# Decoder layer with a mixture of experts on one core: VectorE's order in the first mixture pass, and the last sum read from PSUM

## The chip, the cores and the metric

The kernel runs on one core of one Trainium2 chip. The metric is the device time of one execution in microseconds (us). Five engines run their own queues in order and wait for each other by semaphores: TensorE (PE, with PEld for the loading of its weights), VectorE (DVE), ScalarE (ACT), GpSimd (POOL) and SyncE (SP), which issues most of the transfers.

## The reference

8 sequences of 512 tokens, 256 features. Self attention, cross attention, then a mixture of experts, each followed by a layer norm of input plus output. The last third is what the change touches:

```python
scores = softmax(x @ gate_w.T)                       # 8 experts
topk_w, topk_idx = top_k(scores, 2); topk_w /= topk_w.sum(-1)
pos = cumsum(one_hot(topk_idx.reshape(-1)), 0) - 1   # place of a token in its expert's queue
keep = pos_tok < capacity                            # 1.25 * N * K / E
y  = sum over experts of comb * (silu(x @ wg.T) * (x @ wu.T)) @ wd.T
sh = silu(x @ ws_gate.T) * (x @ ws_up.T) @ ws_down.T # two shared experts' worth, 512 wide
x = layernorm(x + y + sh)
```

## The kernel before

After the two attention layers (up to about 1251 us of the span) `moe_phase` works in three parts.

**The first mixture pass** walks over the 8 blocks (sequences) i = 0 to 7. Each block is a "job" of the first shared expert. TensorE turns the block's tokens (`turn`, into `ps_t`, in two halves f), multiplies for gate and up in two halves c (`gate_up(i, 0)`, `gate_up(i, 1)`, 12 matmuls of 512 columns each, into `ps_gu`), makes the routing scores of the next block (`score(i + 1)`, 24 matmuls of 8 columns) and then `down(i)` (24 matmuls of 256 columns, into `ps_dn`). All values are split into a high and a low part: ScalarE writes the high part (`x_hi`, `h_hi`, `split_hi` for weights), VectorE the rest (`x_lo`, `h_lo`, `split_lo`). The weights of three more experts are split in blocks 1 to 3 by VectorE and behind blocks 0 to 2 by ScalarE. For half c VectorE forms `product(i, c)` (silu(gate) times up), ScalarE `h_hi(i, c)`, VectorE `h_lo(i, c)`; only then may `down` run. `choose(i + 1)` on VectorE is the choice of two experts from the scores (19 small steps, with one exponential on ScalarE between two table loads), and `place(i)` turns the counts that TensorE made (`count`) into places in the experts' queues (10 small steps, semaphore `step_done`). GpSimd then scatters the block's tokens to `slots_x` in memory by 8 indirect transfers, and SP loads a later block into the same buffer (`HELD` = 3 buffers). ScalarE's `keep(i)` copies `ps_dn` to `ym`, from where SP stores it.

**The chunks.** Jobs 8 and 9 are the second shared expert for blocks 6 and 7. Then 40 chunks of 256 gathered tokens follow; the first (`chunk_turn(0)`) needs the scatter of block 7 and its load into `xs`. TensorE puts `chunk_turn(0)` between `down(8)` and `down(9)`.

**The last pass** is jobs 10 to 15 (`LATE` = 10), the second shared expert for blocks 0 to 5, and the final layer norm of 8 sums, n = 0 to 7 (n = 0 and 1 belong to jobs 8 and 9, n = 2 to 7 to jobs 10 to 15). GpSimd's `both(n)` adds two loaded parts into `totals`; VectorE's `moments(n)` adds the job's output in two halves ("pairs", 128x512 each), takes statistics of each 256 columns and aggregates them; GpSimd computes the scale and shift (`rstd`, `shift`), ScalarE's `norm(n)` applies them and SP stores. GpSimd runs `both(n + 3)` right behind the scale of n. In VectorE's queue `moments` stands behind each half job from (12, 1) on. TensorE's queue is gate_up(j, 0), gate_up(j, 1), down(j - 1). Each half of `down(j)` waits until ScalarE's `keep` has emptied that half of `ps_dn`:

```python
                        after(pe, ym_done, out_of_job(j - 1, pair) if j else 0)
```

## Time and profile before

| | |
|---|---|
| median of 3 runs | 1666.03 us (1665.53 to 1670.77) |
| profiled execution | 1674.12 us, span 1672.3 us, mean granted clock of TensorE 0.935 |
| PE busy | 1497.8 us (90%) |
| DVE busy | 1127.0 us (67%) |
| ACT busy | 922.1 us (55%) |
| POOL busy | 449.3 us (27%) |
| chain that ended last | PE 18%, DVE 4%, issue 1%, ACT 1% of the span |

Busy time is a share over the whole span. The change touches the stretches from 1265 to 1402 us (first pass) and from 1610 us to the end (last pass), and only the rows of these say what it is worth. The profiled execution's own time is 1.8 us above its span and 8.1 us above the median of the runs.

### The profile page before, as it was taken

To read this page: it belongs to the slowest core of one execution; us is meant where nothing else is said; L and a number is where in the kernel's file an instruction comes from. 1 tells how busy PE (TensorE), PEld (TensorE's weight loads), DVE (VectorE), ACT (ScalarE), POOL (GpSimd) and SP (SyncE) were. 2 spreads that over 40 slices of the span, in tenths; PEclk is the share of its full clock that TensorE was granted. 3 is DMA by queue.
4 is the path that set the end of the run, shared out by engine and by line. 5 is a ranking of instruction groups with operands and counts; after the bars stand their busy time and mean duration, and the time that the engine had idled before them with its cause. 6 is when DMAs were issued, how large, how long until landed. Compare 5 with 4: busy or idle time off the path is not lost. (4 is left out here: it accounts for less than half of the span.)

```text
span 1672.3 us, 27139 instructions
## 1 busy us (share of the span) xinstructions
PE 1497.8 (90%) x8424; PEld 991.3 (59%) x8424; DVE 1127.0 (67%) x2282; ACT 922.1 (55%) x1710; POOL 449.3 (27%) x412
## 2 busy tenths in 40 slices
PE   3887999999999999999999999986957899999993
PEld 2435555546555555554655555544437789999983
DVE  4736678778778868877877887845625664555557
ACT  3352566656656656665666665660624554555544
POOL 6013032013014103201301310101002543666664
PEclk8696999999999999999999999997967789999997
DMA  3616545554356455545535644506104534777662
GB/s 117 114 55 120 121 94 109 115 108 106 65 126 116 78 115 105 107 106 111 111 65 136 123 67 97 106 2 120 21 24 150 184 121 139 131 155 149 122 189 101
DMA packets 103990, 179.80 MB, mean 108 GB/s; under 512 B 14144, under 2 KB 59840, under 8 KB 101824
## 3 DMA queue, kind: packets, MB, share of 16 engines
q1 hardware_dynamic: 89280, 159.09, 42.5%
q0 software_dynamic: 14592, 19.41, 6.5%
q8 instruction: 42, 0.69, 0.2%
q14 instruction: 76, 0.62, 0.2%
HBM read 98.09 MB, written 79.30 MB: 106 GB/s over the span
## 5 line engine op out<-in xcount | busy, mean ns | idle before, releaser
L509 DVE TENSOR_REDUCE nm<-ps_max 128x1 f32<-128x512 f32 x1024 | 647.4, 682 | 179.3 <-PE ps_max L694 164.7
L469 ACT ACTIVATE prob<-ps_sc 128x512 f32<-128x512 f32 x1024 | 557.9, 597 | 333.6 <-PE ps_sc L707 319.2
L707 PE MATMUL ps_sc<-qk 128*128 128x512 f32 x1024 | 454.4, 447 | 47.1 <-DMA qk<-mst 30.6
L694 PE MATMUL ps_max<-qk 96*128 96x512 f32 x1024 | 428.8, 428 | 25.5 <-DVE nm L509 13.8
L707 PEld LDWEIGHTS ps_sc<-qk 128*128 128x128 f32 x1024 | 194.9, 192 | 342.6 <-ACT prob L469 276.3
L724 PE MATMUL ps_out<-prob,va 128*32 128x512 f32 x2048 | 277.7, 615 | 3.1 <-ACT prob L469 2.8
L694 PEld LDWEIGHTS ps_max<-qk 96*128 96x128 f32 x1024 | 204.4, 200 | 77.5 <-DVE nm L509 42.0
L1453 PE MATMUL ps_gu<-x2f,we 128*128 128x256 f32 (+1 forms) x1344 | 219.6, 318 | 4.0 <-ACT sg L1121 2.4
L1453 PEld LDWEIGHTS ps_gu<-x2f,we 128*128 128x128 f32 x1344 | 187.2, 189 | 20.7 <-ACT sg L1121 2.8
L351 POOL TENSOR_TENSOR rstd<-mv,eps 128x2 f32<-128x2 f32 x32 | 6.3, 197 | 652.6 <-DVE mv L578 652.6
L1453 PE MATMUL ps_dn<-we,hf 128*128 128x256 f32 x864 | 127.4, 305 | 22.3 <-DVE hf L1353 22.3
L1453 PEld LDWEIGHTS ps_dn<-we,hf 128*128 128x128 f32 x864 | 121.3, 213 | 23.9 <-DVE hf L1353 23.3
L614 PE MATMUL ps_job<-xf,w 128*128 128x512 f32 x288 | 81.8, 423 | 24.1 <-POOL xf L326 18.9
L724 PEld LDWEIGHTS ps_out<-prob,va 128*32 128x32 f32 x2048 | 40.6, 108 | 94.7 <-issue 68.6
L614 PE MATMUL ps_job<-w,cf 128*128 128x256 f32 x576 | 82.0, 295 | 5.7 <-DVE cf L495 3.6
L1045 POOL DMA_INDIRECT slots_x<-x2in,scat x64 | 65.4, 1022 | 79.7 <-issue 42.1
L614 PEld LDWEIGHTS ps_job<-w,cf 128*128 128x128 f32 x576 | 78.2, 201 | 9.6 <-DVE cf L495 4.2
L614 PEld LDWEIGHTS ps_job<-xf,w 128*128 128x128 f32 x288 | 55.6, 201 | 39.1 <-issue 20.6
L335 POOL TENSOR_TENSOR res<-res,trig 128x512 f32<-128x512 f32 x32 | 41.0, 1280 | 139.6 <-DVE res L526 139.6
L1059 POOL DMA_INDIRECT sums<-ys,dest x40 | 62.2, 1555 | 48.2 <-DVE dest L1389 24.9
L1059 POOL DMA_INDIRECT x<-ys,dest x40 | 62.0, 1550 | 31.4 <-ACT ys L1188 17.3
L326 POOL TENSOR_TENSOR xf<-raw,xf 128x1024 fp32r<-128x1024 f32 x8 | 21.4, 2674 | 146.7 <-ACT xf L381 146.7
(145 smaller groups left out, 1491.5 us busy)
## 6 DMA issues: line engine op xcount, KB each, us to landing
qk<-hbm_self SPq DMA_DIRECT2D x192, 128.0 KB, 5.3
hbm_self<-stage SPq DMA_DIRECT2D x16, 1024.0 KB, 4.0
qk<-hbm_cq SPq DMA_DIRECT2D x96, 128.0 KB, 5.0
qk<-hbm_ck SPq DMA_DIRECT2D x96, 128.0 KB, 5.5
slots_x<-zeros SPq DMA_DIRECT2D x8, 1360.0 KB, 5.8
xs<-slots_x SPq DMA_DIRECT2D x40, 272.0 KB, 3.9
weraw<-w_moe SPq DMA_DIRECT2D x11, 768.0 KB, 4.4
hbm_ck<-stage SPq DMA_DIRECT2D x8, 1024.0 KB, 4.4
```

Of the source, the lines that this page charges most:

```text
L326: nc.gpsimd.tensor_tensor(out, value, high.bitcast(F32), ALU.subtract).then_inc(lo_done[kind], 1)
L335: nc.gpsimd.tensor_tensor(rot[:, c, :], rot[:, c, :], trig[:, 1, :], ALU.mult) \
L351: nc.gpsimd.tensor_tensor(rstd[:, at, :], mv[:, at, 1:2], eps[:, at, :], ALU.add) \
L469: nc.scalar.activation(prob[:, s % 2, j, :], ps_sc[:, (HG * s + j) % NSC, :], ACT.Exp, scale=HD ** -0.5).then_inc(exp_done[a], 1)
L509: nc.vector.tensor_reduce(nm[:, g % 2, r:r + 1], ps_max[:, n % NMX, :], axis=AX.X, op=ALU.max, negate=True).then_inc(max_done[a], 1)
L614: ins = nc.tensor.matmul(out, l(a), r(b), start=(n == 0 and k == 0), stop=(n == len(pairs) - 1 and k == len(parts) - 1))
L694: nc.tensor.matmul(ps_max[:, n % NMX, :], qk[0:96, 0, h, P * c:P * c + P], qk[0:96, 1, h, :], start=True, stop=True).then_inc(smax_done[a], 1)
L707: nc.tensor.matmul(ps_sc[:, n % NSC, :], qk[:, 1, h, P * c:P * c + P], qk[:, 0, h, :], start=True, stop=True).then_inc(st_done[a], 1)
L724: ins = nc.tensor.matmul(ps_out[32 * j:32 * j + 32, :], va[:, a, c, HG * g + j, :], prob[:, s % 2, j, :], start=(c == 0), stop=(c == TT - ...
L1045: nc.gpsimd.indirect_dma_start(rows_x, bass.IndirectOffsetOnAxis(ap=scat[:, q, c, t:t + 1], axis=0), xin[:, q, t, :], None, bounds_check=P ...
L1059: nc.gpsimd.indirect_dma_start(x2 if j // NCH else sums, bass.IndirectOffsetOnAxis(ap=dest[:, c, t:t + 1], axis=0), ys[:, c, t, :], None, ...
L1453: ins = nc.tensor.matmul(o, l(a), r(b), start=(n == 0 and k == 0), stop=(n == len(pairs) - 1 and k == len(parts) - 1))
```

## The change

In the first pass `place(i)` is cut in two on VectorE: `take_counts(i)` (two small steps that read the counts from PSUM) stays behind `h_lo(i, 0)`, and the other nine steps, with `split_lo` behind them, come after `product(i, 1)` and `h_lo(i, 1)`.

In the last pass a table sets where `moments(n)` and `norm(n)` stand. n = 4 to 7 no longer go through ScalarE and `ym`: VectorE adds `ps_dn` straight into `totals`, and `down(j)` for j = 13 to 15 waits for that add of job j - 1 (`total_done`) where it waited for ScalarE's copy (`ym_done`).

```diff
+MOMENTS_AT = {(12, 0): 0, (12, 1): 1, (13, 0): 2, (13, 1): 3, (14, 0): 4, (15, 0): 5, (15, 1): 6}
+NORM_AT = {(12, 1): 0, (13, 0): 1, (13, 1): 2, (14, 0): 3, (14, 1): 4, (15, 1): 5}
...
-                    if pair == 0 and j >= B + MARGIN:
-                        act.wait_ge(total_done, 2 * (j - MARGIN - B + 1))
...
-                    n = 2 * (j - LATE - 2) + c - 2
-                    if n >= 0 and c == 0:
-                        norm(n)
-                if j > LATE:
-                    keep(j - 1)
-                if n >= 0 and c == 1:
-                    norm(n)
-            keep(NJ - 1)
+                    if c == 1 and LATE < j <= B + MARGIN:
+                        keep(j - 1)
+                    if (j, c) in NORM_AT:
+                        norm(NORM_AT[j, c])
...
                 h_lo(i, 0)
+                take_counts(i)
+                product(i, 1)
+                h_lo(i, 1)
                 place(i)
                 if 1 <= i < 4:
                     split_lo(i, i % 2, i)
-                product(i, 1)
-                h_lo(i, 1)
...
+                    if n < MARGIN:
+                        dve.wait_ge(ym_done, out_of_job(B + n, pair))
+                        nc.vector.tensor_tensor(mine, mine, ym[:, (B + n) % MARGIN, 2 * pair:2 * pair + 2, :],
+                                                ALU.add).then_inc(total_done, 1)
+                    else:
+                        dve.wait_ge(dn_done, of_job(B + n, pair))
+                        flat = mine.rearrange("p t d -> p (t d)")
+                        nc.vector.tensor_tensor(flat, ps_dn[:, pair, :], flat, ALU.add).then_inc(total_done, 1)
...
-                    n = 2 * (j - LATE - 2) + c - 1
-                    if n >= 0:
-                        moments(n)
+                    if (j, c) in MOMENTS_AT:
+                        moments(MOMENTS_AT[j, c])
...
-                        after(pe, ym_done, out_of_job(j - 1, pair) if j else 0)
+                        if j > B + MARGIN:
+                            pe.wait_ge(total_done, 2 * (j - 1 - B) + pair + 1)
+                        else:
+                            after(pe, ym_done, out_of_job(j - 1, pair) if j else 0)
```

VectorE's queue in a block of the first pass, before, from `h_lo(i, 0)` on (`h<-ps_gu,sg` is `product`, `hf<-h,hf` is `h_lo`, the rows of `r`, `prod`, `scat` and `tok` are `place`):

```order
L1353 TENSOR_TENSOR hf<-h,hf 128x512
L1322 TENSOR_TENSOR r<-ps_t,carry 128x32
L1323 TENSOR_TENSOR carry<-carry,ps_t 128x8
L1324 TENSOR_SCALAR r<-r 128x32
L1325 TENSOR_TENSOR r<-r,idx 128x32
L1326 TENSOR_TENSOR r<-r 128x32
L1327 TENSOR_TENSOR prod<-choice,r 128x64
L1331 TENSOR_REDUCE place<-prod 128x8
L1335 CAST scat<-place 128x8
L1337 COPY x2in<-r 128x4x8
L1338 COPY x2in<-tok 128x4
L1339 TENSOR_SCALAR tok<-tok 128x4
```

The same place of the queue in the changed kernel (its lines are numbered anew, L1317 and L1318 are the two steps that read the counts):

```order
L1353 TENSOR_TENSOR hf<-h,hf 128x512
L1317 TENSOR_TENSOR r<-ps_t,carry 128x32
L1318 TENSOR_TENSOR carry<-carry,ps_t 128x8
L1349 TENSOR_TENSOR h<-ps_gu,sg 128x512
L1353 TENSOR_TENSOR hf<-h,hf 128x512
L1324 TENSOR_SCALAR r<-r 128x32
```

`product(i, 1)` and `h_lo(i, 1)` now stand ahead of nine of the steps; before they stood behind all of them.

VectorE's queue in the last pass of the changed kernel, from `product(14, 0)` to `h_lo(15, 0)` (`totals` are the sums, `st` and `mv` the statistics); before, a `moments` with `totals<-totals,ym` stood behind each of the pairs `h`, `hf`, behind (14, 1) too:

```order
L1349 TENSOR_TENSOR h<-ps_gu,sg 128x512
L1353 TENSOR_TENSOR hf<-h,hf 128x512
L1432 TENSOR_TENSOR totals<-ps_dn,totals 128x512
L1435 BN_STATS st<-totals 128x6 x2
L1432 TENSOR_TENSOR totals<-ps_dn,totals 128x512
L1435 BN_STATS st<-totals 128x6 x2
L1440 BN_AGGR mv<-st 128x2 x4
L1349 TENSOR_TENSOR h<-ps_gu,sg 128x512
L1353 TENSOR_TENSOR hf<-h,hf 128x512
L1349 TENSOR_TENSOR h<-ps_gu,sg 128x512
L1353 TENSOR_TENSOR hf<-h,hf 128x512
```

The rows are `moments(4)`, then the half jobs (14, 1) and (15, 0) with nothing between them. `moments(0)` to `moments(3)`, which still read `ym`, each stand one half job earlier than before.

## Rows read from the trace of the kernel before

**Rows 1.** Groups by line of ScalarE, 1030 to 1680 us: shape, count, busy us, mean ns.

```profile
L1108 ACT ACT_TABLE_LOAD x15 | 19.2, 1283 | 0.3
L1139 ACT ACTIVATE ym<-ps_dn 128x512 f32<-128x512 f32 x32 | 18.7, 595 | 20.9 <-PE ps_dn L1453 20.9
L1099 ACT ACTIVATE we<-weraw 128x1536 fp32r<-128x1536 f32 x10 | 14.8, 1475 | 0.0
```

**Rows 2.** Timeline of block 1: start, us, engine, line; in brackets idle before, releaser.

```profile
1286.92 3.04 PE L1453 MATMUL ps_gu<-x2f,we 128*128 128x512 f32 x12
...
1289.34 0.17 DVE L1324 TENSOR_SCALAR r<-r 128x32 f32<-128x32 f32 x1
...
1291.34 1.76 DVE L1252 TENSOR_TENSOR we<-weraw,we 128x1536 fp32r<-128x1536 f32 x1
...
1295.00 0.18 DVE L1290 TENSOR_REDUCE r<-ps_t 128x4 f32<-128x32 f32 x1
...
1295.14 5.02 PE L1453 MATMUL ps_dn<-we,hf 128*128 128x256 f32 x24 [2.61 <-DVE hf L1353]
...
1299.80 0.19 DVE L1313 TENSOR_TENSOR r<-r 128x32 f32<-128x32 f32 x1
...
1302.76 0.69 DVE L1259 TENSOR_TENSOR x2f<-ps_t,x2f 128x512 fp32r<-128x512 f32 x1 [2.76 <-ACT x2f L1105]
```

**Rows 3.** Timeline of block 4, which splits no weights.

```profile
1337.84 3.05 PE L1453 MATMUL ps_gu<-x2f,we 128*128 128x512 f32 x12
...
1342.26 0.69 DVE L1349 TENSOR_TENSOR h<-ps_gu,sg 128x512 f32<-128x512 f32 x1
...
1344.39 4.38 PE L1453 MATMUL ps_dn<-we,hf 128*128 128x256 f32 x24 [0.94 <-DVE hf L1353]
...
1349.99 0.69 DVE L1259 TENSOR_TENSOR x2f<-ps_t,x2f 128x512 fp32r<-128x512 f32 x1 [0.71 <-ACT x2f L1105]
```

**Rows 4.** Windows: us, busy (instructions) of PE, PEld, DVE, ACT, POOL, granted clock, DMA.

```profile
1357.50:1358.00 0.50, 0.50 (x4) 0.50 (x4) 0.01 (x1) 0.46 (x1) 0.42 (x1) 0.50 0.34 119
...
1646.00:1650.00 4.00, 0.00 (x0) 0.00 (x0) 3.06 (x10) 0.67 (x2) 1.90 (x5) 1.00 0.27 108
1650.00:1657.00 7.00, 0.00 (x0) 0.00 (x0) 6.03 (x13) 3.91 (x8) 4.49 (x5) 0.57 0.19 75
```

**Rows 5.** Timeline from the places of block 7 to the first chunk.

```profile
1386.30 0.17 DVE L1339 TENSOR_SCALAR tok<-tok 128x4 f32<-128x4 f32 x1
...
1399.02 12.34 SPq L969 DMA_DIRECT2D xs<-slots_x  x8
...
1401.76 0.16 DVE L1385 SCALAR_TENSOR_TENSOR extra<-xs,spare 128x2 f32<-128x2 f32 x1 [0.51 <-DMA xs<-slots_x]
...
1401.78 0.66 PE L1544 MATMUL ps_t<-ident,xs 128*128 128x128 f32 x4
```

**Rows 6.** Timeline of the last pass.

```profile
1612.33 2.86 POOL L1072 TENSOR_TENSOR totals<-totals,x2in 128x1024 f32<-128x1024 f32 x1
...
1613.07 0.69 DVE L1349 TENSOR_TENSOR h<-ps_gu,sg 128x512 f32<-128x512 f32 x1 [0.15 <-PE ps_gu L1453]
...
1614.46 1.28 DVE L1353 TENSOR_TENSOR hf<-h,hf 128x512 fp32r<-128x512 f32 x1 [0.70 <-ACT hf L1130]
...
1619.31 0.69 DVE L1349 TENSOR_TENSOR h<-ps_gu,sg 128x512 f32<-128x512 f32 x1
...
1622.70 2.11 DVE L1425 TENSOR_TENSOR totals<-totals,ym 128x512 f32<-128x512 f32 x1
...
1642.88 2.99 PE L1453 MATMUL ps_dn<-we,hf 128*128 128x256 f32 x24
...
1654.88 0.69 DVE L1349 TENSOR_TENSOR h<-ps_gu,sg 128x512 f32<-128x512 f32 x1
...
1657.01 4.99 PE L1453 MATMUL ps_dn<-we,hf 128*128 128x256 f32 x24 [11.14 <-DVE hf L1353]
...
1662.66 0.69 DVE L1425 TENSOR_TENSOR totals<-totals,ym 128x512 f32<-128x512 f32 x1 [0.51 <-ACT ym L1139]
```

More of the change, by code:

```diff
@@ L1314, in choose, with take_counts @@
                 assert done[0] == CHOSEN, done
-            def place(i):
-                q, done = i % HELD, [CHOSEN]
-                step = make_step(i, done)
+            def take_counts(i):
+                step = make_step(i, [CHOSEN])
                 dve.wait_ge(cnt_done, i + 1)
@@ L1323, in place @@
                 v.tensor_tensor(carry[:, :, :], carry[:, :, :], counts[:, TT:TT + 1, :], ALU.add).then_inc(ready, 1)
+            def place(i):
+                q, done = i % HELD, [CHOSEN + 1]
+                step = make_step(i, done)
                 step(v.tensor_scalar(past, pos, float(CAP), float(PLACES), ALU.is_ge, ALU.mult))
@@ L1422, in moments @@
                 for pair in range(2):
-                    dve.wait_ge(ym_done, out_of_job(B + n, pair))
                     mine = total(n)[:, 2 * pair:2 * pair + 2, :]
-                    nc.vector.tensor_tensor(mine, mine, ym[:, (B + n) % MARGIN, 2 * pair:2 * pair + 2, :], ALU.add) \
-                        .then_inc(total_done, 1)
+                    if n < MARGIN:
[6 more added lines that the diff above has]
+                        nc.vector.tensor_tensor(flat, ps_dn[:, pair, :], flat, ALU.add).then_inc(total_done, 1)
                     dve.wait_ge(total_done, 2 * n + pair + 1)
```

## Prediction

> **What bounds the kernel now.** The page came first: TensorE is busy 90% of the span, but the chain that ended last spreads over TensorE and VectorE in the two stretches that the change touches. So I read the timeline of each stretch and asked at each wait of TensorE who was late. In the first pass `down` waits for VectorE's `h_lo`: 2.61 us in block 1 [rows 2], 0.94 us in block 4 [rows 3]. Between the first pass and the chunks two things are late together: the first chunk's rows land just as TensorE is through with `down(8)`, since VectorE's use of `xs` was released by the load at 1401.76 and TensorE turned it at 1401.78 [rows 5]. In the chunks TensorE never waits, so what is won ahead of them is kept. In the last pass VectorE is the bound: from 1619.31 to 1654.88 there are five half jobs with a `moments` each, 7.11 us apart, and TensorE then sits idle for 11.14 us before the last `down` [rows 6].
>
> **First pass, what a block is worth.** Call G the end of gate_up(i, 1). In block 1 G is 1286.92 + 3.04 = 1289.96 [rows 2]. Before, `place` and `split_lo` stand ahead of `product(1, 1)`, and `down` starts at G + 5.2. From a `product` to its `down` there are 2.13 us (1342.26 to 1344.39 [rows 3]), so behind G directly `h_lo` is done at G + 2.2. TensorE must first do `score`, 24 thin matmuls that take about 2.7 us: `down` now starts at G + 2.7, 2.5 us earlier in a block with a split. In block 4 G is 1340.89, `down` starts at G + 3.5 [rows 3] and would start 0.9 us earlier.
>
> What is late instead is `choose(i + 1)`. It stood at G + 5.04 in block 1 (1295.00 [rows 2]). Now: `h_lo` done at G + 2.2, nine steps of `place` from 1289.34 to 1291.34, 2.0 us, the split 1.76 us [rows 2], so G + 6.0. Behind its start lie on ScalarE, which waits for it: 0.5 until the exponential can run, 0.2 for it, 1.28 + 0.2 for the table, two copies of 0.6, the weight split of 1.48 [rows 1], `x_hi` at 0.6 like the copies, then VectorE's `x_lo` 0.69: 6.1 us, so `x_lo` ends at G + 12.1. Before it ended at 1303.45, G + 13.5, because the copies waited for the end of the slow `down` (1300.16). TensorE's turn and gate_up(i + 1, 1) hang on `x_lo`. So block 1 gives 1.4 to 1.5 us, not 2.5; block 2 the same. Block 3 has VectorE's split but not ScalarE's behind it: `choose` ends at G + 6.0 + 4.7, `x_lo` at G + 11.4, against a turn at about G + 13.4 (5.2 + 4.9 + 0.3 + 3.05 on TensorE): 2.0 us. Block 0 has no split ahead of its product; by the same chain I take 1.1 us, between the 0.9 and the 1.45. Blocks 4 to 6 are bound by TensorE; `x_lo` there has a slack of over 1 us (it ended at 1350.68, and its turn waits for TensorE's queue, 1344.39 + 4.38 for `down`, 0.3 for the other turn, 3.05 for gate_up(5, 0): 1352.1), which covers the 0.8 us by which `choose` is later. They give 0.9 us each. Sum: 1.1 + 2 x 1.45 + 2.0 + 3 x 0.9 = 8.7 us.
>
> **First pass, the price at its end.** `place(7)` ended at 1386.47, and 15.3 us later its rows were on the chip, through 8 scatters, SP and one load, 1401.76 [rows 5]. It now stands behind a `product` and `h_lo` that wait for G: at G + 4.2 in place of G + 1.6, with G near 1384.85 there. TensorE's work from G to `chunk_turn(0)` is unchanged and was continuous, and `down(9)` is queued behind the turn. The slack is about zero, so TensorE gets a new wait of 2.5 us. First pass net: 6.2 us won.
>
> **Last pass.** Four parts.
> (1) `moments(0)` now starts behind `h_lo(12, 0)`, at 1612.92 (the product at 1613.07 less its 0.15 idle), while GpSimd is in its third `both` from 1612.33 to 1615.19. VectorE's operations with both inputs in SBUF end only with it: `h_lo` took 1.28 us there in place of 0.69 and ended at 1615.74; an add in the middle of the next one took 2.11 in place of 0.69, while a product with one input in PSUM took 0.69 beside it [rows 6]. So the first add ends at 1615.74, and `moments(0)` (7.11 - 2.1 for the half job - 1.42 blocked = 3.6 us, less the add of 0.7) at 1618.7. Before, the half job (12, 1) and `moments(0)` together ended at 1619.31; now the half job is still to come. That costs 1.5 us against the same work.
> (2) Then three slots of 7.11, as before: 1640.0. `moments(4)` and (5) add from PSUM. No row shows that add. The bounds are 0.69 (the product beside GpSimd) and 2.11 (the blocked one) [rows 6]; I take 0.69, as its operands lie like the product's. The Trainium skill, page SBUF — State Buffer, section "Who interferes with whom", says the same: one SBUF input does not contend, two do. This gives 1.42 twice, 2.8 us.
> (3) `down(13)` may overwrite `ps_dn` only behind the adds of `moments(4)`, which stand at slot (14, 0): half job 2.1, add 0.7, so 1642.8. TensorE is through with gate_up(14, 1) at about 1635.1 (its second half, 1.5 us, needs `product(13, 1)`, which runs from 1618.7 + 2 x 7.11 to 1633.6). It idles 7.7 us. Before, an idle stretch from 1646 left the clock at 1.00 for the first 4 us and then let it fall, mean 0.57 over the next 7 [rows 4], and the following `down` took 4.99 us in place of 2.99 [rows 6]. So `down(13)` ends near 1647.8, and gate_up(15, 0) of 3.0 behind it at 1650.8. VectorE is free at 1640.0 + 5.7 + 2.1 = 1647.8: a new wait of 3.1 us for `product(15, 0)`. With the clock up it would be about 1 us.
> (4) From 1650.9: 5.7 for (15, 0) with `moments(5)`, 2.1 for (15, 1): `h_lo(15, 1)` ends at 1658.7 against 1657.0 before. The tail gets shorter: before, the last add ended 6.4 us behind that point (slow `down`, then ScalarE's copy, 1662.66 + 0.69). Now `moments(6)` covers `down(15)`, 3.6, then add, statistics, add, 2.2: 5.8 us.
> Net: 1.7 - 0.6, so 1.1 us lost, which I take as 1.0. The eight ScalarE copies that go move nothing else: ScalarE is not waited for there but for `h_hi`, and `norm` keeps its distance of one half job.
>
> **Sum.** - 8.7 + 2.5 + 1.0 = - 5.2 us against the profiled execution's 1674.12, so 1668.9; the median of the runs lies 8.1 us lower, and the same difference gives 1660.8. A measurement of this kernel tells 0.3%, 5.0 us, from no change, so the forecast lies right at that bound.
>
> **The rivals.**
> *The clock comes back.* With no idle ahead of `down`, and none long enough ahead of `down(13)`, blocks 4 to 6 gain up to 1.5 each until `x_lo` or the counts bind, and the last pass 2.1. For it: in block 4 `down` took 4.38 us, not 5, so the clock was already back in its last part [rows 3]. Against: [rows 4]. Time: 1660.8 - 1.8 - 2.1 = 1657. Chance 0.15.
> *The load is hidden.* If the scatter of block 7 has 2.5 us of air that the rows do not show, the wait at the first chunk is gone: 1658.3. Against: [rows 5], where load and turn are 0.02 us apart. Chance 0.05.
> *The gain goes half-way back.* `down(13)` and gate_up(15, 0) both slow (4.99 + 5), 2 us more; PSUM adds blocked like the others, 2.8 us more; or longer slow stretches in blocks 4 to 6. One of these makes 1663 to 1664, two 1666. Chance 0.20.
> *Slower.* `choose` becomes the block's bound. It starts 0.8 to 0.95 us later behind G in every block. If the next `x_lo` were released by its end, each of seven blocks would be 0.85 us longer and none shorter: 6.0 + 2.5 + 1.0, 1675.5. It decides where ScalarE's `x_hi` is done before `choose` ends. The rows show VectorE waiting 2.76 and 0.71 us for ScalarE at that place [rows 2, 3], so there is air, 0.7 us of it in the blocks without a split. Chance 0.05.
> *As forecast*, 0.55, with 1659 to 1662.5 as its own range.
>
> **The numbers.** 1656.5 holds the clock's return but for its far end, 1665.2 the half-way case but for its end. Faster by over 0.3% (under 1661.0): about six tenths of the forecast's 0.55, all of the first two rivals, 0.53. Slower by over 0.3%: 0.05. The rest, 0.42.
>
> **What will show it.** Right if `down` starts 2.7 us behind gate_up(i, 1) in every block with TensorE not idle; `x_lo` in block 1 ends about 12.1 us behind G; TensorE waits about 2.5 us for `xs` before the first chunk; the four PSUM adds take 0.69 us; and TensorE idles some 7 us ahead of `down(13)`, with VectorE waiting for `product(15, 0)`. Wrong if the `down`s of the first pass turn fast, if ScalarE's chain is not what releases `x_lo`, or if a further wait shows in front of `turn`, where a buffer's load is now 2 to 3 us later against its block.

## The result, and the profile after

In the comparison that the prediction was made for, the changed kernel took 1661.19 us (median of 20 runs, 1656.72 to 1667.5) and the kernel before 1669.15 us (20 runs, 1664.98 to 1674.31): a ratio of 0.9951, 95% interval 0.9938 to 0.9964, 8.0 us less. The forecast was 1660.8 us and 5.2 us less. That the time itself came out within 0.4 us is in part luck: the forecast started from the 1666.03 us of three runs of the kernel before, and its 20 runs beside the changed one gave 1669.15. Repeated in two later comparisons of the same two programs the ratio was 1.0006 (0.9987 to 1.0024) and 1.0014 (0.9997 to 1.0032), with the kernel before at 1679.75 and 1681.00 us. The gain is clear of the scatter in the first comparison and not there in the later ones; most of what follows is about why.

The page of the changed kernel, as far as it answers to the table of before: TensorE now waits for the first chunk's load and for an add of VectorE.

```profile
span 1656.0 us, 27128 instructions
...
PE 1491.3 (90%) x8424; PEld 986.0 (60%) x8424; DVE 1125.6 (68%) x2282; ACT 917.3 (55%) x1702; POOL 447.9 (27%) x412
...
PE ps_gu L1458 10%; PE ps_dn L1458 6%; PE ps_t L1458 1%; PE ps_t L1552 1%; PE ps_t L1468 1%; DVE st L1435 1%; DVE totals L1427 0%; DVE h L1349 0%; ACT hf L1132 0%; POOL slots_x L1047 0%; DVE mv L1440 0%; DVE totals L1432 0%; DMA x2in<-x 0%; DVE we L1248 0%; ACT totals L1221 0%
...
L1458 PE MATMUL ps_dn<-we,hf 128*128 128x256 f32 x864 | 127.0, 305 | 9.4 <-DVE totals L1432 9.4
```

Block 1 on the timeline of the changed kernel (start, us, engine, line; in brackets the idle time before and what ended it), the place of [rows 2]:

```profile
1277.19 3.04 PE L1458 MATMUL ps_gu<-x2f,we 128*128 128x512 f32 x12
1280.07 2.73 PE L1458 MATMUL ps_t<-wg,x2f 128*128 128x8 f32 x24
1282.66 4.61 PE L1458 MATMUL ps_dn<-we,hf 128*128 128x256 f32 x24
...
1280.32 0.69 DVE L1349 TENSOR_TENSOR h<-ps_gu,sg 128x512 f32<-128x512 f32 x1 [0.63 <-PE ps_gu L1458]
...
1286.01 0.18 DVE L1286 TENSOR_REDUCE r<-ps_t 128x4 f32<-128x32 f32 x1
...
1291.13 0.69 DVE L1255 TENSOR_TENSOR x2f<-ps_t,x2f 128x512 fp32r<-128x512 f32 x1 [0.41 <-ACT x2f L1107]
```

gate_up(1, 1) ends at 1280.23 (the point that the prediction calls G). `down` starts 2.4 us behind it with no wait in brackets, where it was 5.2 with a wait of 2.61, and it is still slow, 4.61 us. `choose` starts at + 5.8 and `x_lo` ends at + 11.6. Behind blocks 0 to 2 `x_lo` still waits for ScalarE (0.72, 0.41 and 0.41 us). Behind blocks 3 to 5 it doesn't: it follows the last step of `choose` at once. Behind block 3 TensorE's turn waits 0.82 us for it, behind 4 and 5 it doesn't wait. Block 3's:

```profile
1321.14 0.69 DVE L1255 TENSOR_TENSOR x2f<-ps_t,x2f 128x512 fp32r<-128x512 f32 x1
...
1321.88 0.66 PE L1468 MATMUL ps_t<-ident,x2in 128*128 128x128 f32 x4 [0.82 <-DVE x2f L1255]
```

The end of the first pass, the place of [rows 5]: the last step of `place(7)`, VectorE's and TensorE's first use of `xs`.

```profile
1369.51 0.17 DVE L1339 TENSOR_SCALAR tok<-tok 128x4 f32<-128x4 f32 x1
...
1384.59 0.16 DVE L1386 SCALAR_TENSOR_TENSOR extra<-xs,spare 128x2 f32<-128x2 f32 x1 [2.73 <-DMA xs<-slots_x]
...
1384.61 0.66 PE L1552 MATMUL ps_t<-ident,xs 128*128 128x128 f32 x4 [2.11 <-DMA xs<-slots_x]
```

The last pass, the place of [rows 6]: VectorE's adds, ScalarE's `norm` (L1221) and `silu` (L1123), TensorE's `down`s.

```profile
1595.58 2.90 DVE L1427 TENSOR_TENSOR totals<-totals,ym 128x512 f32<-128x512 f32 x1
...
1624.73 0.68 DVE L1432 TENSOR_TENSOR totals<-ps_dn,totals 128x512 f32<-128x512 f32 x1
...
1625.56 4.38 PE L1458 MATMUL ps_dn<-we,hf 128*128 128x256 f32 x24 [6.26 <-DVE totals L1432]
1629.77 5.76 PE L1458 MATMUL ps_gu<-x2f,we 128*128 128x512 f32 x24
...
1630.62 2.08 ACT L1221 ACTIVATE totals<-totals,shift,rstd 128x256 f32<-128x256 f32 x4 [0.82 <-POOL shift L1091]
1632.60 0.58 ACT L1123 ACTIVATE sg<-ps_gu 128x512 f32<-128x512 f32 x1
...
1633.21 0.69 DVE L1349 TENSOR_TENSOR h<-ps_gu,sg 128x512 f32<-128x512 f32 x1 [2.69 <-ACT sg L1123]
...
1636.04 3.07 PE L1458 MATMUL ps_dn<-we,hf 128*128 128x256 f32 x24 [0.50 <-DVE totals L1432]
...
1641.74 4.59 PE L1458 MATMUL ps_dn<-we,hf 128*128 128x256 f32 x24 [2.64 <-DVE totals L1432]
```

**Where the time went.** All times below are counted from the first memset of the mixture part (`ident`), so that the attention part, which the change doesn't touch and whose length scatters by 9 us between profiles, drops out. In the first pair of profiles gate_up(7, 1) starts at 120.2 us instead of 131.0 (-10.8); from there to the first chunk's turn it is 22.0 instead of 19.8 (+2.2); the chunks and the second pass, to `product(12, 0)`, take 208.5 in both; from there to the end 62.9 instead of 62.0 (+0.9). Together -7.7 us, and the medians differ by 8.0. One profile of each kernel stands behind these figures. How far such a stretch scatters can be read from the later comparisons: where the last pass is the old one, its length is 61.8 to 62.4 us in three profiles, where it is the changed one 62.6 to 63.0 in seven, so its +0.9 is known to about half a microsecond.

### The profile page after: what moved, and what is told of

It is laid out like the page before. It is cut to its first block and busy times, and to the rows that moved or that the text cites. A ratio compares the mean times of both kernels' runs of the same rounds, so it can differ in the third digit from the quotient of the medians.

```text
span 1656.0 us, 27128 instructions
## 1 busy us (share of the span) xinstructions
PE 1491.3 (90%) x8424; PEld 986.0 (60%) x8424; DVE 1125.6 (68%) x2282; ACT 917.3 (55%) x1702; POOL 447.9 (27%) x412
## 5 line engine op out<-in xcount | busy, mean ns | idle before, releaser
L1205 ACT ACTIVATE hf<-h 128x512 fp32r<-128x512 f32 x40 | 25.3, 632 | 64.0 <-DVE h L1407 61.8
```

The lines of the kernel that those rows point to most:

```text
L1205: nc.scalar.activation(hf[:, p, HI, :, 0:CH], h[:, p, :].rearrange("p (c t) -> p c t", c=IC), ACT.Copy).then_inc(hhi_done, 1)
```

## The experiments

Four comparisons in all; in each of the later three the kernels ran on one chip, side by side with the kernel before, 12 runs of each kernel (4 of e7, 5 of e8, 24 or 35 of the kernel before). Which comparison a kernel ran in turned out to matter most, so it stands in the table. "Distance" is the time from the start of gate_up(i, 1) to VectorE's `product(i, 1)`, read at blocks 0 to 6; it is 3.13 where VectorE is free and TensorE's semaphore comes when the product ends.

| kernel | comparison | ratio to the kernel before, 95% | first chunk's turn, us | wait for `xs` | product(12, 0) to end | distances, blocks 0 to 6 |
|---|---|---|---|---|---|---|
| before | 1 | 1 (1669.15 us) | 150.8 | 0 | 62.0 | 4.42 6.10 6.10 6.10 4.42 4.42 4.42 |
| changed | 1 | 0.9951, 0.9938 to 0.9964 | 142.3 | 2.11 | 62.9 | 3.14 3.13 3.14 3.13 3.13 3.13 3.14 |
| e1 first pass only | 2 (1679.44) | 0.9994, 0.998 to 1.0007 | 158.0 | 4.59 | 62.4 | 3.15 4.53 3.56 4.18 5.32 5.16 4.85 |
| e2 last pass only | 2 | 1.0002, 0.9991 to 1.0014 | 161.4 | 1.28 | 62.8 | 4.42 7.90 6.10 6.10 4.52 5.24 4.53 |
| e3 place(7) early | 2 | 0.9991, 0.9973 to 1.0009 | 151.7 | 1.09 | 62.7 | 3.16 4.53 3.46 3.45 3.86 5.83 5.48 |
| e4 two moments | 2 | 0.9985, 0.997 to 1.0 | 160.8 | 4.50 | 62.3 | 3.15 4.45 3.52 5.56 3.15 6.32 4.81 |
| r1 changed again | 3 (1679.75) | 1.0006, 0.9987 to 1.0024 | 158.2 | 3.72 | 63.0 | 3.14 3.14 3.14 3.51 3.92 6.37 6.88 |
| r2 before again | 3 | 1.0005, 0.9988 to 1.0022 | 159.6 | 1.38 | 61.8 | 4.42 7.06 6.39 6.43 4.90 4.53 4.53 |
| e5 job 12 over ScalarE | 3 | 1.001, 0.9992 to 1.0027 | 155.4 | 3.22 | 63.8 | 3.15 4.36 3.44 3.52 3.14 6.18 6.14 |
| e6 three repairs | 3 | 0.997, 0.9956 to 0.9985 | 151.8 | 2.30 | 63.2 | 3.16 4.49 3.47 3.46 3.86 5.82 5.44 |
| r3 changed, third | 4 (1681.00) | 1.0014, 0.9997 to 1.0032 | 160.9 | 4.51 | 62.7 | 3.16 4.61 4.27 5.05 4.72 5.86 4.33 |
| r4 three repairs again | 4 | 0.9984, 0.9968 to 1.0 | 160.4 | 1.43 | 63.3 | 3.15 4.63 3.61 5.04 5.45 5.96 7.09 |
| e7 one scatter in eight | 4 | 0.9869, 0.9854 to 0.9883 | 142.4 | 0 | 62.6 | 3.16 3.14 3.14 4.05 4.68 3.13 3.13 |
| e8 score in one part | 4 | 0.9967, 0.9951 to 0.9983 | 157.4 | 5.92 | 62.6 | 3.15 3.14 5.05 5.09 5.46 7.31 6.46 |

One thing goes with the wait for `xs` in every row. Where it is 2.30 us or less, the stretch behind it, from the first chunk's turn to `product(12, 0)`, takes 208.3 to 208.5 us. In the six profiles where it is 3.22 us or more (e1, e4, e5, e8, r1, r3) it takes 209.8 to 210.9. TensorE doesn't wait in that stretch in any of them. What differs is its granted clock right behind the wait, 0.50 to 0.61 over the first 2.5 us in the six and 1.00 in the other eight (columns as in [rows 4]; first r3 with a wait of 4.51 us, then e6 with 2.30):

```profile
1403.40:1406.00 2.60, 2.60 (x13) 2.60 (x14) 1.28 (x7) 0.60 (x1) 0.00 (x0) 0.54 1.03 343
...
1399.60:1402.00 2.40, 2.40 (x21) 2.40 (x22) 1.25 (x7) 1.06 (x3) 0.00 (x0) 1.00 1.01 374
```

So the longer waits cost 1.3 to 2.4 us more than they last, and shortening one saves that too.

### e1 and e2: each half of the change alone

e1 is the kernel before with only the first pass's new order, e2 the changed kernel with the old order of the first pass:

```diff
                 h_lo(i, 0)
                 take_counts(i)
-                product(i, 1)
-                h_lo(i, 1)
                 place(i)
                 if 1 <= i < 4:
                     split_lo(i, i % 2, i)
+                product(i, 1)
+                h_lo(i, 1)
```

> The kernel before with the first-pass edit alone. My theory: all of the gain is made here. From the start of the mixture part (GpSimd's first memset) to the first chunk's turn 142 to 144 us in place of 150.8, a wait of about 2 us for xs ahead of that turn, the last pass (from product(12, 0) to the end) 62.0 us as before; time 8 to 9 us under the kernel before, ratio 0.9948. Rival, the last pass carries part of the gain (PSUM adds): this kernel is only 4 to 6 us faster, 0.997. Rival, the gain over my sum was the luck of slow stretches in the profiled execution: the first part then takes 144 to 145 us here and the ratio is 0.996.

> The changed kernel with VectorE's first pass in the old order. My theory: no gain left, 0.5 to 1.5 us slower than the kernel before, ratio 1.0003 to 1.001; first part 150.8 us, from product(12, 0) to the end 62.9 us in place of 62.0, with TensorE idle 6 us ahead of down(13) and VectorE 2.7 us for product(15, 0). Rival, the last pass gives part of the gain: ratio 0.998 and 60 to 61 us.

Neither half moves the median. For the last pass alone that is near what its profile says: 62.8 us, as in the whole change (62.9), against 62.0. For the first pass it is a miss: 0.9994 where the first comparison had given 7.7 us to the two halves together. Its trace is not that of the first comparison either: the first chunk comes at 158.0, not 142.3. e2's first chunk comes at 161.4 where 150.8 was expected. So either the halves need each other, or something else differs. That question led to the repeats below.

### e3 and e4: two of the prices

e3 puts `place(7)` alone back ahead of `product(7, 1)`:

```diff
                 take_counts(i)
+                if i == B - 1:
+                    place(i)
                 product(i, 1)
                 h_lo(i, 1)
-                place(i)
+                if i < B - 1:
+                    place(i)
```

> The changed kernel, but in block 7 alone the places are worked out ahead of product(7, 1), as before the change. My theory: the wait of 2.1 us for xs ahead of the first chunk is nothing but place(7) being late, so it goes and nothing else moves: 2.0 to 2.2 us faster than the changed kernel, 10 us faster than before (0.994). Rival: the load or the scatter is late for another reason (a queue that is busy), the wait stays at 1 us or more.

The wait for `xs` falls from 4.5 us in the neighbours e1 and e4 to 1.09, and the first chunk is 6.3 and 9.1 us sooner than theirs, more than the wait; the rest (2.8 and 5.7 us) lies in the first pass ahead of block 7, where the three kernels are the same, so it is scatter. 1.09 us of wait stay, which is the rival's sign (1 us or more): `place(7)` was most of the wait there, but not all. The old order itself, in e2 and r2 on that level, waits 1.28 and 1.38. The median is 0.9991 of the kernel before, not told from 1, and the changed kernel wasn't run in this comparison.

e4 puts `moments(0)` behind `h_lo(12, 1)`, together with `moments(1)`:

```diff
-MOMENTS_AT = {(12, 0): 0, (12, 1): 1, (13, 0): 2, ...
+MOMENTS_AT = {(12, 1): (0, 1), (13, 0): (2,), ...
```

> The changed kernel, but moments(0) stands with moments(1) behind h_lo(12, 1), not behind h_lo(12, 0). My theory: the add of moments(0) that took 2.90 us beside GpSimd's third addition takes 0.7 again, h_lo(12, 1) pays 0.6 for it, and moments(1), now within 2 us of moments(0), gets both its adds in before GpSimd's next addition starts: 1.5 + 1.4, so 2.9 us less on VectorE. TensorE's wait ahead of down(13) gets shorter by as much and the stall for product(15, 0) stays: 2.5 to 2.9 us faster than the changed kernel, 0.9932 to before. Rival: other operations get into GpSimd's way instead (h_lo(13, 0)), or ScalarE's norm(0) comes too late for silu(13, 0): 0 to 1.5 us.

The last stretch is 62.3 us, 0.5 less than with the change in comparison 1 (0.3 less than the shortest changed last pass of the table) and not the 2.5 to 2.9 that the theory said. The rival named both ways in which it could be lost. VectorE's timeline in e4 shows where it went:

```profile
1623.70 0.68 DVE L1427 TENSOR_TENSOR totals<-totals,ym 128x512 f32<-128x512 f32 x1
1625.09 0.68 DVE L1427 TENSOR_TENSOR totals<-totals,ym 128x512 f32<-128x512 f32 x1
...
1632.26 0.69 DVE L1349 TENSOR_TENSOR h<-ps_gu,sg 128x512 f32<-128x512 f32 x1 [1.21 <-ACT sg L1123]
1633.65 2.93 DVE L1353 TENSOR_TENSOR hf<-h,hf 128x512 fp32r<-128x512 f32 x1 [0.70 <-ACT hf L1132]
```

The adds are free (0.68 each), but the next `both` of GpSimd (1633.64 to 1636.02) now meets `h_lo(13, 0)`, which takes 2.93 instead of 0.69, and `product(13, 0)` waits 1.21 us for a `silu` that stands behind `norm(0)` on ScalarE. The blocking was moved, not removed.

### r1 and r2: both kernels again

> The changed kernel unaltered, since both of its halves alone came out at 0.9994 and 1.0002 on another chip than the first comparison's 0.9951, and in their traces some gate and up products of the first pass gave their semaphore up to 10 us apart where 1.40 us is the rule of the kernel before and of the changed one. Theory A (the chip or its runs, not the halves): the ratio depends on where this runs; if the kernel before is at 1678 to 1681 us here, the changed one comes out at 0.997 to 1.001, its first chunk's turn starts 150 to 160 us into the mixture part (142.3 in the first comparison), and gaps over 2 us between the two halves of a gate and up product are in its trace. Theory B (the two halves need each other): 0.993 to 0.997 wherever it runs, the first chunk at 141 to 144 us, every gap 1.40.

> The kernel before, unaltered, against itself. Its ratio is 1.000 by both theories, and how far it is from 1 says what this comparison can tell. Theory A: where the kernel before is at 1678 to 1681 us, its trace has gate and up products of the first pass with gaps over 2 us, and its first chunk's turn starts at 158 to 164 us instead of the 150.8 of the first trace. Theory B: 150 to 152 us, and all gaps 1.40.

Theory B is out: the whole change, both halves together, has no gain here, so the halves' needing each other isn't why e1 had none. All signs of theory A came: the ratio, the two places of the first chunk, and two halves of a gate_up whose semaphores came over 2 us apart. On the level of 1680 us the kernel before has its first chunk at 159.6 instead of 150.8, the changed one at 158.2 instead of 142.3: both lose, the changed one more (15.9 against 8.8). One stretch of r1 shows what is late; the engines are TensorE, ScalarE and VectorE in block 6.

```profile
1365.98 0.64 PE L1468 MATMUL ps_t<-ident,x2in 128*128 128x128 f32 x4
...
1366.37 3.06 PE L1458 MATMUL ps_gu<-x2f,we 128*128 128x512 f32 x12
...
1371.08 0.60 ACT L1107 ACTIVATE x2f<-ps_t 128x512 fp32r<-128x512 f32 x1 [5.11 <-remote]
...
1372.10 0.59 ACT L1123 ACTIVATE sg<-ps_gu 128x512 f32<-128x512 f32 x1
...
1373.25 0.69 DVE L1349 TENSOR_TENSOR h<-ps_gu,sg 128x512 f32<-128x512 f32 x1
...
1373.45 5.25 PE L1458 MATMUL ps_t<-wg,x2f 128*128 128x8 f32 x24 [4.03 <-DVE carry L1318]
```

The four transposes are through at 1366.62 by their record. ScalarE, idle for 5.11 us, copies their result from 1371.08. In the changed kernel of comparison 1 the like copy, of block 6 as well, starts 0.03 us behind the recorded end of its transposes, 1349.95:

```profile
1349.31 0.64 PE L1468 MATMUL ps_t<-ident,x2in 128*128 128x128 f32 x4
...
1349.98 0.60 ACT L1107 ACTIVATE x2f<-ps_t 128x512 fp32r<-128x512 f32 x1 [1.42 <-PE ps_t L1468]
1350.47 0.62 ACT L1132 ACTIVATE hf<-h 128x512 fp32r<-128x512 f32 x1
1351.38 0.60 ACT L1123 ACTIVATE sg<-ps_gu 128x512 f32<-128x512 f32 x1 [0.29 <-PE ps_gu L1458]
```

It isn't that TensorE computed late: the semaphore updates in the trace of r1 are at 1371.06 for the transposes, 1371.14 and 1371.21 for the gate and the up half of gate_up(6, 1). Six products of 512 columns lie between the last two, which take 1.39 to 1.41 us in every gate_up of the first pass in comparison 1. They came in one burst, late. The trace shows how general that is. Of the 40 semaphore updates of gate_up up to the first chunk, all 40 stand within 0.02 us of the recorded end of their matmuls in both kernels of comparison 1; in r1 16 do and in r2 22, and the rest are late or missing. TensorE itself then stands for 4.03 us, because `score` waits for `take_counts`, which waits behind `x_lo` on VectorE.

Why the new order loses more can be read in good part from the distances. In the old order `product(i, 1)` stood behind `place` and a split anyway, at 4.42 or 6.10 us, and the semaphore had 1.3 to 3 us to be late in: r2's distances hardly grow (blocks 2 and 3: 6.4 instead of 6.1, block 5 and 6: 4.5 instead of 4.4), though block 1's does. In the new order the product follows at 3.13, with nothing in hand: 6.37 and 6.88 in r1's last two. Up to the start of gate_up(7, 1) r2 is 7.3 us behind the kernel before of comparison 1, and 2.3 of them are growth of its distances; r1 is 14.3 us behind the changed kernel, and 8.2 are. So the distances hold 5.9 of the 7.0 us by which the new order loses more; what else both lose stands in other waits (r1's second block is 3.1 us longer with its distance at 3.14).

### e5 and e6: the wait of down(13), and the repairs together

e5 lets the product of job 12 go through ScalarE and `ym` as before:

```diff
-                    if c == 1 and LATE < j <= B + MARGIN:
+                    if c == 1 and LATE < j <= B + MARGIN + 1:
...
-                    if n < MARGIN:
+                    if n <= MARGIN:
...
-                        if j > B + MARGIN:
+                        if j > B + MARGIN + 1:
```

> The changed kernel with the product of block 12 still copied out by ScalarE and added from SBUF; blocks 13 to 15 are added straight from PSUM. The theory of the prediction (down(13) waits for the add behind moments(4), TensorE stands still for 6.3 us and product(15,0) waits 2.7): down(13) starts without a wait and takes 2.99, product(15,0) waits under 0.6; the add of moments(4)'s second half is held by GpSimd again, 2.1 instead of 0.68 (+1.4). From product(12,0) to the end 61.3 to 61.8 instead of 62.9, 0.9993 of the changed kernel. Rival (the end hangs on VectorE's moments, which only move): 62.7 to 63.1.

The stretch takes 63.8 us, more than the rival said. ScalarE's, VectorE's and TensorE's rows of e5:

```profile
1649.23 2.08 ACT L1223 ACTIVATE totals<-totals,shift,rstd 128x256 f32<-128x256 f32 x4 [0.82 <-POOL shift L1091]
1651.21 0.57 ACT L1123 ACTIVATE sg<-ps_gu 128x512 f32<-128x512 f32 x1
...
1651.82 0.69 DVE L1351 TENSOR_TENSOR h<-ps_gu,sg 128x512 f32<-128x512 f32 x1 [2.68 <-ACT sg L1123]
...
1654.65 5.46 PE L1460 MATMUL ps_dn<-we,hf 128*128 128x256 f32 x24 [5.17 <-DVE totals L1434]
```

down(13) no longer waits and takes 2.99, as expected. But `product(15, 0)` waits 2.68 us all the same, with TensorE's gate_up(15, 0) long done (its second half began at 1640.71 and took 1.66): the `silu` stands behind `norm(4)` on ScalarE. And TensorE's idle time has only gone to down(14), 5.17 us. So TensorE's lateness is not the only thing that makes this product wait, and the repair costs one more blocked add (2.05 us) and gives nothing.

e6 is e3, e4 and e5 in one.

> The changed kernel with three repairs: the places of the last block ahead of its second product, as before the change; moments of blocks 0 and 1 both behind product(12,1); the product of block 12 over ScalarE. By the parts: the wait for the slots' rows falls from 2.1 to 1.1 or less (-1.0), moments(0)'s add is free of GpSimd (-0.5 as measured for that edit), block 12 -1.3: 2.8 us under the changed kernel run beside it, 0.9983 of it, with 60.8 to 61.4 from product(12,0) to the end. Rival (the repairs lie behind one another or the scatter between executions is larger): within 1 us of the changed kernel.

> The kernel with the three repairs, once more beside the changed one. If its 1673.94 against 1681.49 us was the repairs' doing, it is again 0.9955 to 0.9985 of the changed kernel; by the parts named before it should be 0.998 to 0.9985. Rival (most of the 7.5 us was scatter): 0.9985 to 1.001 of it.

e6 beat the changed kernel beside it by 7.5 us in comparison 3 (1673.94 and 1681.49), more than its parts explain. In comparison 4 the same program (r4) was 2.4 us faster (1680.84 and 1683.25): 0.9986 of it, at the edge where the rival begins, with runs that overlap widely (1670.25 to 1684.06 and 1677.41 to 1690.86). So most of the 7.5 us was scatter, and that the repairs give anything over the changed kernel is shown in one comparison of two. They beat the kernel before in both, by 0.997 and 0.9984, the second with an interval that touches 1. The last stretch is no shorter (63.2 and 63.3, where 60.8 to 61.4 was expected), so what they give lies ahead of it, where of the three only e3's edit is: 2.3 and 1.4 us of wait for `xs` against 3.7 and 4.5, and 208.5 us behind it against 209.8 and 210.1. Of the versions tried here that do all the work, e6 has the lowest ratio on the level of 1680 us; in the condition of comparison 1 it was not run.

### r3, e7 and e8: the changed kernel a third time, fewer scatters, a shorter score

> The changed kernel once more. Theory A of the repeat before (the chip decides): where the kernel before is under 1672 us the ratio is 0.993 to 0.997, product(i,1) follows the start of gate_up(i,1) after 3.13 to 3.15 us in every block of the first pass, and the first chunk's turn is at 141 to 144 us; where it is over 1677 us the ratio is 0.998 to 1.001, the distance grows from 3.1 to 5 or 7 us over the blocks, and the first chunk's turn is at 155 to 160 us. Rival (chance between executions, whatever the chip): no such tie between the level of the kernel before and the distance.

The level of the kernel before was 1681 us. Theory A's picture came again, each number a little past or beside what was named: the ratio is 1.0014 (0.998 to 1.001 named), the first chunk comes at 160.9 (155 to 160), and the distances lie between 3.16 and 5.86 without growing steadily. The three comparisons on the 1680 level ran on three different chips, and no second one came out at 1670, so chance between single executions, the rival, is unlikely.

e7 leaves one of the eight indirect scatters of a block:

```diff
-        PER_BLOCK = 16 * 2 * TT
+        PER_BLOCK = 16
...
-                for t in range(TT):
-                    for c in range(2):
+                for t in range(1):
+                    for c in range(1):
```

> The changed kernel with one of each block's eight indirect scatters left, so most rows never reach their slots (that part of the computation is left out); all else runs. Theory: TensorE's semaphores come late in the first pass because they share a way with GpSimd's scatters and their descriptors. Then, on a chip where the changed kernel shows distances of 5 to 7 us from gate_up(i,1) to product(i,1), they are 3.13 to 3.5 here, and the first chunk's turn comes 10 us or more sooner than in the changed kernel beside it. Rival (TensorE itself, or the chip's supply, is late): distances of 4 to 7 us stay and the first chunk moves by under 4 us, which is the wait for the slots' rows. On a chip without late semaphores: 3.13 in both, and 2 us less by the wait for the slots' rows.

The first chunk comes at 142.4 us, 18.5 us sooner than in r3 beside it; the wait for `xs` is 4.5 of that. Five of the seven distances are 3.13 to 3.16. The median is 23.6 us under r3's. With seven of eight scatters gone the kernel is back where comparison 1 had it with all of them (142.3). Blocks 3 and 4 have longer distances (4.05 and 4.68), because in them gate_up itself took 3.95 and 4.59 us, partly at the low clock; the semaphores are on time there too. All 40 updates of gate_up up to the first chunk stand within 0.02 us of the recorded ends, where r3 beside it has 21. So it is by the scatters that TensorE's semaphores are late, when they are late. Which part of them does it (GpSimd's issuing, the writes to memory or the semaphore updates of the transfers) one edit that takes all three away can't tell.

e8 makes `score` a third as long, with the high parts alone:

```diff
-                    ins = products(logits[:, t, :], ...
+                    for f in range(FC):
+                        ins = nc.tensor.matmul(logits[:, t, :], xf[:, i, HI, f, P * t:P * t + P], wg[:, HI, f, :],
```

> The changed kernel with one of the three partial products of the scores (8 matmuls of 8 columns instead of 24; the two low parts are left out). Theory of the prediction's clock reading (the score's thin matmuls and what stands around them, not idle time, go before each fall of the granted clock): down stays at or near 3.0 us in four or more of seven blocks, where the changed kernel's took 4.35 to 5.5; each such block is 1.4 to 1.8 us shorter beside the 1.8 us of 16 matmuls at 0.11, and the first chunk's turn comes 8 to 15 us sooner. Rival (the clock falls at set distances whatever the score does): down 4.3 to 5.5 in six of seven, and blocks shorter by at most what TensorE was the bound for, 0 to 1.8 us each.

Inconclusive on the clock. With its short `score` TensorE idled 1.4 to 3.1 us ahead of `down` in blocks 0 to 4, r3 beside it 0 to 1.6, so the edit moved two things at once. `down` took 3.14 us in blocks 0 and 1 and 4.8 to 5.4 behind them, neither the four of my theory nor the rival's one. And r1, the changed kernel itself with its whole score, also had 3.12 us in blocks 0 and 1, where the same program took 4.53 and 4.61 in comparison 1 and 4.33 and 4.64 in r3. From block 2 on the late semaphores lengthen e8 too. The kernel is 4.7 us faster than r3 by the medians of 5 and 12 runs; 3.4 us of that lie ahead of `product(0, 1)`, in the first `score` at the low clock (20.8 us instead of 24.3).

## Why the prediction was right, and where it wasn't

The forecast was 5.2 us less for comparison 1, the measurement 8.0. The three terms of the sum (8.7 won, 2.5 and 1.0 lost) measured 10.8, 2.2 and 0.9, and each came by the mechanism named for it. One wait had a second cause that the forecast had ruled out, and the condition under which all of it holds was not seen.

**First pass, a block's worth: right in kind, 2.1 us too small.** Forecast for blocks 0 to 6: 1.1, 1.45, 1.45, 2.0, 0.9, 0.9, 0.9. Measured by the starts of gate_up(i + 1, 1): 1.12, 1.89, 1.75, 2.17, 0.84, 1.97, 1.05. `down` starts behind `score` without a wait in all seven. The mis-sized terms are blocks 1 and 2, where I put `x_lo` at G + 12.1 and it was at G + 11.6 (in block 1 `choose` started at G + 5.8, not 6.0, and the chain from there took 5.8 us, not 6.1), and block 5: before, its `down` took 5.48 us, now 4.61. The forecast treated the slow `down` as one length, so 0.9 of the 2.1 us is luck.

**The slow downs stay: right here.** They took 4.35 to 5.47 us in all seven blocks, with TensorE never idle ahead of them. The window just ahead of block 6's `down` and its first microsecond, columns as in [rows 4]:

```profile
1354.60:1355.18 0.58, 0.58 (x8) 0.58 (x7) 0.55 (x3) 0.58 (x1) 0.00 (x0) 1.00 0.64 225
1355.18:1356.18 1.00, 1.00 (x7) 1.00 (x7) 0.86 (x5) 0.51 (x2) 0.00 (x0) 0.62 0.01 4
```

TensorE is busy throughout and the granted clock falls inside the second; it is 0.50 from 1358.0 to 1358.5. The Trainium skill (page TensorE: Matmul & The Clock Gate, section "HAM oscillation") names idle gaps as what lets it fall; here it fell without one in TensorE's records, whose ends are modelled. Behind the long waits for `xs` the traces agree with the page: there the clock was low after TensorE had stood idle. What decides it stays open: the same program kept the clock up over blocks 0 and 1 in r1.

**The price at the end of the first pass: right.** 2.5 us forecast, TensorE waited 2.11, and 14.9 us lay between `place(7)` and the use of its rows, against the 15.3 of [rows 5]. In comparisons 2 to 4 the wait is longer, 3.2 to 4.6 us (5.9 in e8), and the chunks behind it lose 1.3 to 2.4 us more by the clock, a cost that the forecast didn't have.

**Last pass: the sum right (1.0 forecast, 0.9 measured), one step wrong.** Part (1): the blocked add of `moments(0)` is there, 2.90 us. Part (2): the four PSUM adds took 0.67 to 0.68 us, one of them beside GpSimd's `both` from 1624.83 to 1627.19; adds from SBUF with two inputs there took 2.05 to 2.90 beside `both`. That agrees with what the Trainium skill, page SBUF — State Buffer, section "Who interferes with whom", says of one and of two SBUF inputs. Part (3): TensorE idled 6.26 us ahead of down(13) (7.7 forecast), and `product(15, 0)` waited 2.69 (3.1 forecast). But the step "so `down(13)` ends near 1647.8, and gate_up(15, 0) of 3.0 behind it ... a new wait of 3.1 us for `product(15, 0)`" named only one of two causes. TensorE was late as foretold: the semaphore of gate_up(15, 0)'s second half came at 1632.75, which by itself would have held the product to about 1632.8 (an estimate; elsewhere it follows such an update by less than 0.1 us). It started at 1633.21, because its `silu` stood behind `norm(4)`, 2.08 us on ScalarE. e5 took TensorE's lateness away and the wait stayed at 2.68, by the `norm` alone. The two are level within half a microsecond, so removing one gives nothing. What failed is the sentence that `norm` "keeps its distance": a distance to the products in the order of one engine says nothing of when its inputs come, and `norm(4)` waits for GpSimd's `shift`, which comes behind `moments(4)`. Moving `norm(4)` behind that `silu` was not tried.

**The rivals.** The clock didn't come back, and the load wasn't hidden. The condition of "slower", that `x_lo` is released by the end of `choose`, was met behind three of the six blocks, 3 to 5; for block 3 the forecast's own sum had it so. It was a sign of being wrong in the prediction's list, and yet nothing was lost by it but 0.82 us behind block 3: behind 4 and 5 TensorE's own queue was the later one, as the forecast said. It is the price of that rival that didn't come, not its condition.

**What no part of the prediction held** is that the gain needs punctual semaphores. The sum took each semaphore at the moment the trace of one execution gave. In the later comparisons the kernel before was 0.6 to 0.7% slower than in the first, the changed one 1.2 to 1.3%, and what was left between them lay between -0.13 and +0.32%. The forecast's own case "no difference that a measurement tells" was reached there by another way than any rival. Shown: the lateness is there in both kernels, in the first pass, and goes when most scatters are left out; most of what the new order loses more stands in the distances. Argued, not shown: that the old order is steadier because its products come later anyway, and that the 8.0 us would be back on any chip once the semaphores come on time. The kernel before with one scatter in eight, beside e7, would have tested both; it was not run. Nor were the two halves of the change run in the condition of comparison 1, so what each gave there rests on one profile of each kernel. Open: comparisons 2, 3 and 4 ran on three different chips; which one the first ran on isn't recorded, so whether its chip or a passing condition was the better one can't be told, nor what in the scatters delays the semaphores.

## What to carry to other kernels

A reordering that takes all slack between a product and its reader is worth what the trace says only where the semaphores come on time; look at one distance (start of the matmuls to start of the reader) over all iterations, and in more than one profile, before its gain is booked. Where an idle engine and a busy queue end level, removing the one gives nothing: e4 and e5 both moved a stall to the next `norm` or the next `both`. Work at the end of a phase whose result the next phase loads (here `place(7)`) belongs ahead of work that only its own engine needs, even where the rest of the loop goes the other way: the waits of e3, e6 and r4 (1.1 to 2.3 us against 3.2 to 4.6) speak for it, though no median shows it alone. And a wait of TensorE costs more than its length once the clock has fallen by its end.

## What was not expected of the hardware

Three of four comparisons had TensorE's semaphores up to 4.9 us late (in e8; 4.4 in r1) in the stretch where GpSimd issues indirect scatters, and then several at once. The traces of these three differ from the first's in another way too: records are missing. The 64 scatters raise their semaphores 1024 times in the traces of comparison 1 (16 times each, as the Trainium skill says, page DMA: Bandwidth & Descriptors, section "Why a DMA increments its semaphore by 16 and not by 1"); in r1, r2 and r3 only 248, 317 and 253 of these updates are recorded, and TensorE's gate_up semaphore has 127, 137 and 132 of 145. The page of a run then has no landing time for the chunk loads. First the kernel before in comparison 1, under its DMA issues:

```profile
xs<-slots_x SPq DMA_DIRECT2D x40, 272.0 KB, 3.9
```

and the same line in r2, the same program in comparison 3:

```profile
xs<-slots_x SPq DMA_DIRECT2D x40, 272.0 KB
```

In e7 the 128 updates of its eight scatters are all recorded, but the load's line is without a landing there too, and gate_up's semaphore has 137 of 145, as in r2, though up to the first chunk none is late. So missing records go with these comparisons and are no measure of the lateness; the times of the updates that are there, against the ends of their matmuls, are.

An engine's record alone doesn't show this: TensorE's rows have their ends modelled and look the same, 3.04 to 3.06 us a gate_up, in punctual and late blocks. It is the reader's idle time that tells, and the time of the semaphore's update.

GpSimd's `both` took 2.36 us (at 1624.83) beside VectorE's adds from PSUM and 2.80 and 2.87 (1610.62, 1603.53) beside those from SBUF. In e4 it took 2.38 with `h_lo` held for its whole length, so the holding alone doesn't lengthen it.
